# Maxima handed to the scores by halves, and the weighing moved between two pairs of matmuls, in an attention of 16 heads

## The chip, the cores and the metric

The kernel runs on one core of a Trainium2 chip. The metric is the device time of one launch in microseconds, the median of several runs; lower is better.

## What is computed

The program is a network of four blocks over x of 4 batches x 1024 tokens x 128 features: a gated linear recurrence with a feed-forward layer, a mixture of experts, an attention block, and a second attention block with a mixture of experts. The change touches the two attention blocks alone, which have one shape:

```python
q, k = rope(proj(Wq, bq)), rope(proj(Wk, bk))     # 4 batches, 16 heads, 1024 tokens, 8 features a head
v = proj(Wv, bv)
scores = einsum('bhtd,bhsd->bhts', q, k) / sqrt(8)
attn = softmax(scores, axis=-1)                   # over all 1024 keys, no mask
out = einsum('bhts,bhsd->bhtd', attn, v)          # 4 x 16 x 1024 x 8
y = out.reshape(B, T, 128) @ Wo + bo
```

Everything is float32 at the borders. Queries and keys are split into a high and a low part (three products of 8 features) and held as 25 rows, the 25th of which is the maximum of a query's scores on the query side and -1 on the key side, so that one matmul gives score minus maximum.

## The kernel before, in words

An attention block (called a layer here, there are two) has a stage for each batch, `attention_inputs`, which makes the 25-row parts of queries and keys and stores them to `qk_parts` in HBM, and then one stage, `attention`, for all batches. That stage works on 16 groups (`GROUPS`), each of 4 heads of one batch. A group's parts are loaded by SP into one of 4 slots of `qs` and `ks` (`load`, eight DMAs).

For each group two things are computed by TensorE (PE):

- **Maxima.** A unit (`max`, one head and one tile of 128 queries, 32 units a group) is two matmuls of 128 queries against 512 keys each (line 923), into a pair of PSUM banks. VectorE (DVE) reduces the 128 x 1024 scores to a column of `mx` (line 1043). There are two such pairs of banks, taken in turn by all work in the list `fills`: fill n waits until fill n-2 has been read (`ring`). When a group's maxima are there, `turn_max` transposes `mx` (line 930), DVE copies it to `m_row` (line 1048), and SP copies that to the 25th rows of `qs` (`store_maxima`, line 884).
- **Steps.** A step s takes one tile of 128 keys and 512 queries (a half) for the four heads: a group is 16 steps, 8 for each half. `score(s, j)` is one matmul (line 959) into one of 3 score banks; ScalarE (ACT) takes the exponential (line 1023) into `p`; `weigh(s)` multiplies the four heads' `p` by the values and a column of ones (line 969, four matmuls beside each other in column groups). The score matmul n waits until the exponential n-3 is done (line 957), the weighing of step s-1 until all exponentials of step s-1 are done (line 965).

The order on PE is written out by hand. Ahead of the steps stands a lead of `LEAD` units, the last 8 fills of it with an extra matmul (`WARM`, line 976). Then each step has two units, `one` and `two`, taken apart into their two matmuls and put between the scores; heads 0 and 1 lie in partitions 0 to 63, heads 2 and 3 in 64 to 127, so a score matmul and a unit's matmul of the other half of the partitions can run beside each other. The order of a step before is

```python
score(s,0) one(0) score(s,1) one(1) score(s,2) weigh(s-1) two(0) score(s,3) two(1) [turns]
```

where heads 0 and 1 of the scores stand next to unit heads 2 or 3 (`one`), and scores 2 and 3 next to unit heads 0 or 1 (`two`).

The turns are further fills of a single bank, behind a step's units, by the table `fill_plan`: `turn_max` of group g in step 16g-3; `turn_out` (four transposes of the weighed half, line 934, after ACT copied it out by `copy_out`, line 1008) in steps 16g+9 and 16g+17; at a batch's end two `turn_o` and, two steps later, two `project` (line 947), which DVE adds up (line 1063). `copy_out` of a half stands on ACT behind the third exponential of the first step of the next half and waits for the last weighing of the half.

At the stage's start SP waits for `parts_stored`, all stores of `qk_parts`, then loads three groups.

Of the kernel before, what the change touches and what calls it, by code (L numbers as in the profile page):

```python
# [5 lines left out]
F32 = mybir.dt.float32  # L6
# [8 lines left out]
P = 128  # L15
# [7 lines left out]
GH = 4  # L23
# [795 lines left out]
M_BANK, NM = 3, 2  # L819
O_BANK = 7  # L820
STEPS = NH * NT
LEAD = 40
WARM = 8
GROUPS = B * NG

# [1 line left out]
def fill_plan():  # L827

    plan = [[] for _ in range(GROUPS * STEPS + 8)]
    first = [("max", *divmod(u, UN)) for u in range(LEAD)]  # L830
    first.insert(UN, ("turn_max", 0, 0))
    for u in range(LEAD, GROUPS * UN):
        s = (u - LEAD) // 2
        plan[s].append(("max", *divmod(u, UN)))
    for g in range(GROUPS):
        if g:
            plan[STEPS * g - 3].append(("turn_max", g, 0))
        for h in range(NH):
            plan[STEPS * g + NT * (h + 1) + 1].append(("turn_out", g, h))
        if g % NG == NG - 1:  # L840
            s = STEPS * (g + 1)
            plan[s + 3] += [("turn_o", g // NG, h) for h in range(NH)]
            plan[s + 5] += [("project", g // NG, h) for h in range(NH)]
    return first, plan


def attention(nc, t, w, layer, a):
# [14 lines left out]
    with stage(nc, "loaded0", "loaded1", "loaded2", "loaded3", "row0", "row1", "filled", "used", "turned",  # L862
# [5 lines left out]
        @block.sync  # L868
        def _(sp):
            def load(g):  # L870
                if g >= NKF:
                    sp.wait_ge(scored, GH * STEPS * (g - NKF + 1))
                b, h0, n = g // NG, (g % NG) * GH, g % NKF
                for j in range(GH):
                    r = slice(GR * j, GR * j + ROWS_QK)
                    sp.dma_start(a["qs"][r, n, :].bitcast(F32), t["parts"][b, 0, h0 + j, :, :]).then_inc(loaded[n], 16)
                    sp.dma_start(a["ks"][r, n, j % KM, :].bitcast(F32), t["parts"][b, 1, h0 + j, :, :])\
                        .then_inc(loaded[n], 16)

            def store_maxima(g):  # L880
                sp.wait_ge(turned, g + 1)
                for j in range(GH):
                    r = GR * j + ROWS_QK - 1
                    sp.dma_start(a["qs"][r:r + 1, g % NKF, :].bitcast(F32).rearrange("r (i c) -> r i c", c=P),
                                 a["m_row"][NT * j:NT * (j + 1), g % 2, :].bitcast(F32)).then_inc(row[g % 2], 16)

            sp.wait_ge(t["parts_stored"], PART_STORES * 16 * B * (layer + 1))
            for g in range(3):
                load(g)
            for g in range(GROUPS):  # L890
                store_maxima(g)
                if g + 3 < GROUPS:
                    load(g + 3)

        @block.tensor
        def _(pe):
# [11 lines left out]
            def fill(f, parts=(0, 1)):  # L908
                kind, g, u = f
                n = number[f]  # L910
                if parts[0] == 0:
                    assert made[0] == n
                    made[0] += 1
                    bank = ring(n)
                else:
                    bank = M_BANK + 2 * (n % NM)
                if kind == "max":
                    i, j = place(u)
                    if u == 0 and parts[0] == 0:
                        pe.wait_ge(loaded[g % NKF], 16 * 2 * GH * (g // NKF + 1))  # L920
                    for h in parts:
                        r = slice(j // KM * KT, (j // KM + 1) * KT)
                        last = pe.matmul(psum[:, bank + h, :], a["qs"][r, g % NKF, i * P:(i + 1) * P],  # L923
                                         a["ks"][r, g % NKF, j % KM, h * HALF:(h + 1) * HALF], start=True, stop=True)
                    if parts[-1] == 1:
                        last.then_inc(filled, 1)
                elif kind == "turn_max":
                    done = number["max", g, UN - 1] + 1
                    pe.wait_ge(used, done - sum(by_act[:done]))
                    pe.transpose(psum[0:UN, bank, 0:P], a["mx"][:, g % 2, :], t["ident"][:, :]).then_inc(filled, 1)  # L930
                elif kind == "turn_out":
                    pe.wait_ge(out_copied, NH * g + u + 1)
                    for i in range(TPH):
                        last = pe.transpose(psum[:, bank, i * P:(i + 1) * P], a["o_raw"][:, u, i * P:(i + 1) * P],
                                            t["ident"][:, :])
                    last.then_inc(filled, 1)
                elif kind == "turn_o":
                    done = number["turn_out", NG * g + NG - 1, u] + 1
                    pe.wait_ge(used, done - sum(by_act[:done]))
                    for i in range(TPH):  # L940
                        last = pe.transpose(psum[:, bank, i * P:(i + 1) * P], a["o"][:, u * TPH + i, :], t["ident"][:, :])
                    last.then_inc(filled, 1)
                else:
                    pe.wait_ge(o_copied, NH * g + u + 1)
                    for i in range(TPH):
                        c = (u * TPH + i) * P
                        last = pe.matmul(psum[:, bank, i * P:(i + 1) * P], t["y_t"][:, c:c + P], w.att[layer][5],
                                         start=True, stop=True)
                    last.then_inc(filled, 1)

            def score(s, j):
                g, (h, i) = s // STEPS, divmod(s % STEPS, NT)
                n = GH * s + j
                if s % STEPS == 0 and j == 0:
                    pe.wait_ge(row[g % 2], 16 * GH * (g // 2 + 1))
                if n >= NS:
                    pe.wait_ge(exped, n - NS + 1)
                r = slice(j // KM * KT, (j // KM + 1) * KT)
                pe.matmul(psum[:, S_BANK + n % NS, :], a["ks"][r, g % NKF, j % KM, i * P:(i + 1) * P],  # L959
                          a["qs"][r, g % NKF, h * HALF:(h + 1) * HALF], start=True, stop=True).then_inc(scored, 1)  # L960
# [16 lines left out]
            for s in range(nsteps):  # L977
                todo = list(plan[s])
                one = todo.pop(0) if todo and todo[0][0] == "max" else None
                two = todo.pop(0) if todo and todo[0][0] == "max" else None  # L980
                score(s, 0)
                if one:
                    fill(one, (0,))
                score(s, 1)
                if one:
                    fill(one, (1,))
                score(s, 2)
                if s:
                    weigh(s - 1)
                if two:  # L990
                    fill(two, (0,))
                score(s, 3)
                if two:
                    fill(two, (1,))
                for f in todo:
                    fill(f)
# [6 lines left out]
        def _(act):  # L1003
# [6 lines left out]
            def copy_o(b):  # L1010
                for h in range(NH):
# [2 lines left out]
                    act.activation(t["y_t"][:, h * HALF:(h + 1) * HALF], psum[:, bank, :], ACT.Copy)\  # L1014
                        .then_inc(o_copied, 1)

            for s in range(nsteps):
                for j in range(GH):
                    n = GH * s + j
# [13 lines left out]
        def _(dve):  # L1033
            recips = 0
            for n, (kind, g, u) in enumerate(fills):
# [3 lines left out]
                dve.wait_ge(filled, n + 1)  # L1039
                if kind == "max":  # L1040
                    i, j = place(u)
                    c = NT * j + i
                    dve.tensor_reduce(a["mx"][:, g % 2, c:c + 1], psum[:, bank:bank + 2, :].rearrange("p a d -> p (a d)"),  # L1043
                                      AX.X, ALU.max).then_inc(used, 1)
                elif kind == "turn_max":
                    if g >= 2:
                        dve.wait_ge(row[g % 2], 16 * GH * (g // 2))
                    dve.tensor_copy(a["m_row"][:, g % 2, :], psum[0:UN, bank, 0:P]).then_inc(turned, 1)
                    dve.wait_ge(turned, g + 1)
                    dve.sem_inc(used, 1)  # L1050
                elif kind == "turn_out":
                    out = psum[:, bank, :].rearrange("p (i j c) -> p i j c", i=TPH, j=GH)
# [18 lines left out]
def build(nc, x_in, cols_in, rows_in, gates_in, ident_in, cos_in, sin_in, w0_in, wo_in, w1_in, w2_in,  # L1071
          att_in, gate_in, consts_in, moe0_in, moe1_in, out):
    with ExitStack() as ctx:
        names = {}

        def sb(name, shape, dt=F32, where=ctx):
            names[name] = names.get(name, 0) + 1
            return where.enter_context(nc.sbuf_tensor(f"{name}_{names[name]}", shape, dt))
# [147 lines left out]
        for layer in range(2):  # L1226
            with ExitStack() as scope:
                a = {}
                t["v_ext"] = sb("v_ext", [P, B * NT, HEADS * VE + VW - VE], where=scope)
                a["qs"] = sb("qs", [P, NKF, L], F32R, where=scope)  # L1230
                a["ks"] = sb("ks", [P, NKF, KM, L], F32R, where=scope)
                target = (x_all, n_all)[layer]
                with ExitStack() as inner:
                    t["cos"], t["sin"] = sb("cos", [P, L], where=inner), sb("sin", [P, L], where=inner)
# [32 lines left out]
                a["p"] = sb("p", [P, NP, HALF], where=scope)  # L1267
                a["o_raw"] = sb("o_raw", [P, NH, HALF], where=scope)
                a["o"] = t["x2"]
                a["mx"] = sb("mx", [P, 2, UN], where=scope)  # L1270
                a["m_row"] = sb("m_row", [UN, 2, P], F32R, where=scope)
                a["rs"] = sb("rs", [P, 2, TPH, GH], where=scope)
                a["sum"] = [view(target, b) for b in range(B)]
                attention(nc, t, w, layer, a)

# [96 lines left out]
```

## Time and profile before

| | us |
|---|---|
| median of 3 runs | 2943.95 |
| lowest and highest | 2941.54, 2946.24 |
| the profiled execution's own time | 2944.78 |
| its span, first to last instruction | 2943.5 |
| mean granted TensorE clock over the span | 0.867 |
| PE busy | 2323.2 (79%) |
| DVE busy | 2053.8 (70%) |
| ACT busy | 1479.5 (50%) |
| POOL busy | 503.9 (17%) |

The two attention stages cover about 793 to 1616 us and 1724 to 2547 us of the span. In the profile PEld is the loading of weights, which runs beside the matmuls; SPq is SP's queue, with a row for each DMA that it issues. A row's time is from its start to its end; instructions on one engine overlap in their pipelines, so that a period is read from start to start. A release in brackets names what ended an engine's idle time. A row of several instructions that overlap is merged (x2, x8).

### The profile page before, as it was taken

The page shows a single profiled execution, that of the slowest core. Times are in us where ns is not written, and L with a number is a line of the kernel's source. Part 1 is how long each engine was busy: PE and PEld are TensorE (multiplying, and loading weights), DVE is VectorE, ACT ScalarE, POOL GpSimd, SP SyncE. Part 2 cuts the span into 40 slices and gives each one's busy share as a digit, 9 for nine tenths or more (in the row PEclk, how much of TensorE's full clock was granted, in tenths as well). Part 3 has the DMA queues.
Part 4 walks back from the last instruction along what each step waited for, and adds up shares of the span by engine and source line. Part 5 has one row for each costly group of instructions (what it writes and reads, how often), then busy time and mean ns, then how long its engine had stood idle before and what let it go on. Part 6 is the DMA issues. An engine that isn't in the chain of part 4 may idle for free. (4 is left out here: it accounts for less than half of the span.)

```text
span 2943.5 us, 37846 instructions
## 1 busy us (share of the span) xinstructions
PE 2323.2 (79%) x13096; PEld 1285.4 (44%) x13096; DVE 2053.8 (70%) x3485; ACT 1479.5 (50%) x2898; POOL 503.9 (17%) x410
## 2 busy tenths in 40 slices
PE   6888856933399999999998559999999999639920
PEld 5667745721144444344443224444444443239920
DVE  6667657635578888888881667888888887266635
ACT  4443320411117777777777104777777777513510
POOL 2223301756400000000000320000000000005644
PEclk9999965966659999999999757999999999857965
DMA  4000010343300000000000320000000000201211
GB/s 165 0 0 0 0 35 18 99 69 114 115 25 12 23 17 19 24 12 24 12 1 5 125 90 12 24 20 16 23 12 24 12 12 1 79 22 50 69 49 50
DMA packets 65302, 109.11 MB, mean 37 GB/s; under 512 B 11120, under 2 KB 45040, under 8 KB 64880
## 3 DMA queue, kind: packets, MB, share of 16 engines
q1 hardware_dynamic: 56176, 88.60, 8.9%
q0 software_dynamic: 8960, 18.37, 2.9%
q8 instruction: 95, 1.56, 0.2%
q14 instruction: 71, 0.58, 0.1%
HBM read 64.46 MB, written 41.94 MB: 36 GB/s over the span
## 5 line engine op out<-in xcount | busy, mean ns | idle before, releaser
L1043 DVE TENSOR_REDUCE mx<-psum 128x1 f32<-128x1024 f32 x1024 | 1216.0, 1220 | 273.4 <-PE psum L923 273.4
L1023 ACT ACTIVATE p<-psum 128x512 f32<-128x512 f32 x2048 | 1086.5, 599 | 493.1 <-PE psum L959 486.4
L959 PE MATMUL psum<-qs,ks 64*128 64x512 f32 x2048 | 838.4, 453 | 13.5 <-ACT p L1023 13.0
L923 PE MATMUL psum<-ks,qs 64*128 64x512 f32 x2048 | 689.4, 461 | 81.7 <-DVE mx L1043 44.1
L923 PEld LDWEIGHTS psum<-ks,qs 64*128 64x128 f32 x2048 | 312.3, 195 | 565.8 <-DVE mx L1043 425.2
L969 PE MATMUL psum<-p,v_ext 128*32 128x512 f32 x4096 | 547.8, 607 | 1.4 <-ACT p L1023 1.4
L959 PEld LDWEIGHTS psum<-qs,ks 64*128 64x128 f32 x2048 | 368.6, 185 | 242.3 <-ACT p L1023 212.3
L157 PE MATMUL psum<-ident,xn 128*128 128x128 f32 x160 | 44.3, 454 | 264.1 <-DVE xn L125 219.8
L575 ACT ACTIVATE hid<-psum,stage 128x128 f32<-128x128 f32 x448 | 132.5, 367 | 181.4 <-PE psum L545 181.4
L519 POOL DMA_INDIRECT x_in<-n_rows,token_of x152 | 167.1, 1100 | 251.0 <-POOLq L78 183.7
L649 POOL COPY n_all<-xn 128x1024 f32 x4 | 4.2, 1040 | 883.4 <-DVE xn L132 883.4
L1261 POOL MEMSET v_ext<- 128x5344 f32 x2 | 9.1, 4552 | 839.7 <-POOLq L78 839.7
L615 POOL DMA_INDIRECT back<-answers,slot_of x128 | 132.8, 1037 | 100.0 <-issue 51.8
L157 PEld LDWEIGHTS psum<-ident,xn 128*128 128x128 f32 x160 | 29.4, 190 | 275.8 <-DVE xn L125 223.7
L545 PE MATMUL psum<-x_t,stage 128*128 128x128 f32 x896 | 137.4, 290 | 9.1 <-DVE x_t L584 6.2
L598 DVE COPY stage<-ew 128x642 f32 (+1 forms) x152 | 95.7, 630 | 69.2 <-DVE y_out L590 64.3
L969 PEld LDWEIGHTS psum<-p,v_ext 128*32 128x32 f32 x4096 | 81.0, 108 | 139.3 <-issue 119.4
L555 PE MATMUL psum<-stage,hid 128*128 128x128 f32 x896 | 126.3, 277 | 0.6 <-ACT hid L575 0.6
L545 PEld LDWEIGHTS psum<-x_t,stage 128*128 128x128 f32 x896 | 114.2, 195 | 25.5 <-DVE x_t L584 23.9
L229 PE MATMUL psum<-y_high,w_high 128*128 128x512 f32 x256 | 106.6, 416 | 20.5 <-PEq L78 20.5
L138 ACT ACTIVATE std<-var 128x8 f32<-128x8 f32 (+1 forms) x29 | 6.1, 210 | 219.8 <-DVE var L110 195.7
L555 PEld LDWEIGHTS psum<-stage,hid 128*128 128x128 f32 x896 | 113.6, 194 | 1.0 <-ACT hid L575 1.0
(171 smaller groups left out, 2378.2 us busy)
## 6 DMA issues: line engine op xcount, KB each, us to landing
qs<-qk_parts SPq DMA_DIRECT2D x128, 100.0 KB
ks<-qk_parts SPq DMA_DIRECT2D x128, 100.0 KB
answers<-y_out SPq DMA_DIRECT2D x152, 64.0 KB, 1.5
qk_parts<-qh SPq DMA_DIRECT2D x16, 512.0 KB, 4.5
qk_parts<-kh SPq DMA_DIRECT2D x16, 512.0 KB, 4.4
ew<-in_moe SPq DMA_DIRECT2D x1, 5136.0 KB, 18.1
ew<-in_moe SPq DMA_DIRECT2D x1, 4624.0 KB, 14.0
n_rows<-xn SPq DMA_DIRECT2D x8, 512.0 KB, 3.2
```

Of the source, the lines that this page charges most:

```text
L229: last = pe.matmul(psum[:, n % BANKS, :], a[:, m, c * P:(c + 1) * P], t[y][:, h * HALF:(h + 1) * HALF], start=(k == 0), stop=(k == 2))
L519: pool.indirect_dma_start(t["x_in"][:, i % NX, :], None, t["n_rows"], bass.IndirectOffsetOnAxis(ap=t["token_of"][:, i:i + 1], axis=0))\
L545: last = pe.matmul(psum[:, 2 + i % 2, f * P:(f + 1) * P], t["stage"][:, i % NST, W1 + f * P:W1 + (f + 1) * P], t["x_t"][:, i % 2, :], star ...
L555: last = pe.matmul(psum[:, 4 + i % 2, 0:P], t["hid"][:, i % 2, f, :], t["stage"][:, i % NST, W2 + f * P:W2 + (f + 1) * P], start=(f == 0), ...
L575: act.activation(t["hid"][:, i % 2, f, :], psum[:, 2 + i % 2, f * P:(f + 1) * P], func, bias=t["stage"][:, i % NST, B1 + f:B1 + f + 1]).th ...
L598: dve.tensor_copy(t["stage"][:, i % NST, :], t["ew"][:, bass.ds(e, 1), :] .rearrange("p a c -> p (a c)")).then_inc(staged, 1)
L615: pool.indirect_dma_start(t["back"][:, b % 2, i, k, :], None, t["answers"], bass.IndirectOffsetOnAxis(ap=t["slot_of"][:, b * NT + i, k:k + ...
L923: last = pe.matmul(psum[:, bank + h, :], a["qs"][r, g % NKF, i * P:(i + 1) * P], a["ks"][r, g % NKF, j % KM, h * HALF:(h + 1) * HALF], sta ...
L959: pe.matmul(psum[:, S_BANK + n % NS, :], a["ks"][r, g % NKF, j % KM, i * P:(i + 1) * P], a["qs"][r, g % NKF, h * HALF:(h + 1) * HALF], sta ...
L969: last = pe.matmul(psum[GR * j:GR * j + VW, O_BANK, :], t["v_ext"][:, b * NT + i, VE * (h0 + j):VE * (h0 + j) + VW], a["p"][:, (GH * s + j ...
L1023: act.activation(a["p"][:, n % NP, :], psum[:, S_BANK + n % NS, :], ACT.Exp, scale=DH ** -0.5)\
L1043: dve.tensor_reduce(a["mx"][:, g % 2, c:c + 1], psum[:, bank:bank + 2, :].rearrange("p a d -> p (a d)"), AX.X, ALU.max).then_inc(used, 1)
```

## The change

What it does:

- `LEAD` goes from 40 to 24 units. The 16 units stand in the steps instead, of which 244 now have two units each, before 236.
- `turn_max`, which was one transpose of 32 columns for a group, is two of 16 columns, one for each half of 512 queries: for the first half in step 16g-3, for the second in step 16g+5, and for group 0's first half in the lead. `m_row` has a place for each half, and each half's row goes by one DMA, before four for a group; each half's first score waits for its own row.
- `weigh(s-1)` stands ahead of `score(s, 2)`, before behind it.
- SP waits for `parts_stored` only ahead of the loads of the last batch, and ACT waits for it at the stage's start instead. `mx`, `m_row` and `rs` are allocated earlier, ahead of the inputs' stage.

```diff
-LEAD = 40
+LEAD = 24
+UH = UN // NH
...
-    first.insert(UN, ("turn_max", 0, 0))
+    first.insert(UH + 2, ("turn_max", 0, 0))
...
-        if g:
-            plan[STEPS * g - 3].append(("turn_max", g, 0))
+        for h in range(NH):
+            if g or h:
+                plan[STEPS * g + NT * h - 3].append(("turn_max", g, h))
...
+                if b == B - 1:
+                    sp.wait_ge(t["parts_stored"], PART_STORES * 16 * B * (layer + 1))
...
-            def store_maxima(g):
-                sp.wait_ge(turned, g + 1)
-                for j in range(GH):
-                    r = GR * j + ROWS_QK - 1
-                    sp.dma_start(a["qs"][r:r + 1, g % NKF, :].bitcast(F32).rearrange("r (i c) -> r i c", c=P),
-                                 a["m_row"][NT * j:NT * (j + 1), g % 2, :].bitcast(F32)).then_inc(row[g % 2], 16)
-
-            sp.wait_ge(t["parts_stored"], PART_STORES * 16 * B * (layer + 1))
+            def store_maxima(g, h):
+                sp.wait_ge(turned, NH * g + h + 1)
+                r = ROWS_QK - 1
+                sp.dma_start(a["qs"][r:P:GR, g % NKF, h * HALF:(h + 1) * HALF].bitcast(F32)
+                             .rearrange("r (i c) -> r i c", c=P), a["m_row"][:, h, :].bitcast(F32)).then_inc(row[h], 16)
+
             for g in range(3):
                 load(g)
             for g in range(GROUPS):
-                store_maxima(g)
+                for h in range(NH):
+                    store_maxima(g, h)
                 if g + 3 < GROUPS:
                     load(g + 3)
...
-                    done = number["max", g, UN - 1] + 1
+                    done = number["max", g, UH * (u + 1) - 1] + 1
                     pe.wait_ge(used, done - sum(by_act[:done]))
-                    pe.transpose(psum[0:UN, bank, 0:P], a["mx"][:, g % 2, :], t["ident"][:, :]).then_inc(filled, 1)
+                    pe.transpose(psum[0:UH, bank, 0:P], a["mx"][:, g % 2, UH * u:UH * (u + 1)], t["ident"][:, :])\
+                        .then_inc(filled, 1)
...
-                if s % STEPS == 0 and j == 0:
-                    pe.wait_ge(row[g % 2], 16 * GH * (g // 2 + 1))
+                if i == 0 and j == 0:
+                    pe.wait_ge(row[h], 16 * (g + 1))
...
-                score(s, 2)
                 if s:
                     weigh(s - 1)
+                score(s, 2)
...
+            act.wait_ge(t["parts_stored"], PART_STORES * 16 * B * (layer + 1))
...
-                    c = NT * j + i
+                    c = UH * (i // TPH) + TPH * j + i % TPH
...
-                    if g >= 2:
-                        dve.wait_ge(row[g % 2], 16 * GH * (g // 2))
-                    dve.tensor_copy(a["m_row"][:, g % 2, :], psum[0:UN, bank, 0:P]).then_inc(turned, 1)
-                    dve.wait_ge(turned, g + 1)
+                    if g:
+                        dve.wait_ge(row[u], 16 * g)
+                    dve.tensor_copy(a["m_row"][:, u, :], psum[0:UH, bank, 0:P]).then_inc(turned, 1)
+                    dve.wait_ge(turned, NH * g + u + 1)
```

The order of the instructions on PE in a plain step of the first layer, from one weighing (psum<-p) to the next; `ks,qs` is a unit's matmul and `qs,ks` a score. Before:

```order
L969 MATMUL psum<-p,v_ext 32x512 x4
L923 MATMUL psum<-ks,qs 128x512
L959 MATMUL psum<-qs,ks 128x512
L923 MATMUL psum<-ks,qs 128x512
L959 MATMUL psum<-qs,ks 128x512
L923 MATMUL psum<-ks,qs 128x512
L959 MATMUL psum<-qs,ks 128x512
L923 MATMUL psum<-ks,qs 128x512
L959 MATMUL psum<-qs,ks 128x512
L969 MATMUL psum<-p,v_ext 32x512 x4
```

And now:

```order
L973 MATMUL psum<-p,v_ext 32x512 x4
L963 MATMUL psum<-qs,ks 128x512
L926 MATMUL psum<-ks,qs 128x512
L963 MATMUL psum<-qs,ks 128x512
L926 MATMUL psum<-ks,qs 128x512
L963 MATMUL psum<-qs,ks 128x512
L926 MATMUL psum<-ks,qs 128x512
L963 MATMUL psum<-qs,ks 128x512
L926 MATMUL psum<-ks,qs 128x512
L973 MATMUL psum<-p,v_ext 32x512 x4
```

The third score of a step stood alone as the last matmul ahead of the weighing; it now follows it and is the first behind it.

The second place is SP's queue between two groups' maxima, in the first layer. Before:

```order
L884 DMA qs<-m_row 1x8x128 x4
L876 DMA qs<-qk_parts 25x1024
L877 DMA ks<-qk_parts 25x1024
```

And now:

```order
L887 DMA qs<-m_row 4x4x128 x2
L880 DMA qs<-qk_parts 25x1024
L881 DMA ks<-qk_parts 25x1024
```

Two DMAs of 4 rows x 4 tiles stand where four of one row stood, and the second of them waits for the second half's maxima, so the load of group g+3 behind it comes eight steps later.

## Rows read from the trace of the kernel before

**Rows 1.** Windows: stretch and length, busy us of each engine, PEclk the granted clock
```profile
805.10:865.60 60.50, 55.21 (x99) 23.53 (x99) 47.64 (x41) 0.00 (x0) 0.00 (x0) 0.50 0.10 39
...
869.70:1609.40 739.70, 711.27 (x4207) 293.96 (x4206) 578.86 (x553) 558.78 (x1055) 0.00 (x0) 1.00 0.04 15
```
**Rows 2.** Timeline of a plain step: start us, duration us, engine, line, what
```profile
1115.59 1.06 PE L969 MATMUL psum<-p,v_ext 128*32 128x512 f32 x8
...
1116.58 0.50 PE L959 MATMUL psum<-qs,ks 64*128 64x512 f32 x1
1116.91 0.39 PE L923 MATMUL psum<-ks,qs 64*128 64x512 f32 x1
...
1117.77 0.50 PE L959 MATMUL psum<-qs,ks 64*128 64x512 f32 x1
1118.20 0.64 PE L969 MATMUL psum<-p,v_ext 128*32 128x512 f32 x4
...
1117.12 0.60 ACT L1023 ACTIVATE p<-psum 128x512 f32<-128x512 f32 x1 [0.53 <-PE psum L959]
...
1117.34 2.35 DVE L1043 TENSOR_REDUCE mx<-psum 128x1 f32<-128x1024 f32 x2 [0.26 <-PE psum L923]
```
**Rows 3.** Timeline of the last step of the first layer, which has no units
```profile
1607.24 1.06 PE L969 MATMUL psum<-p,v_ext 128*32 128x512 f32 x8
1608.23 0.49 PE L959 MATMUL psum<-qs,ks 64*128 64x512 f32 x1
1609.41 0.64 PE L969 MATMUL psum<-p,v_ext 128*32 128x512 f32 x4 [0.69 <-ACT p L1023]
...
1608.76 0.60 ACT L1023 ACTIVATE p<-psum 128x512 f32<-128x512 f32 x1 [0.53 <-PE psum L959]
```
**Rows 4.** Timeline of two steps: ACT copies a half out, ahead of an exponential
```profile
1101.10 1.07 PE L969 MATMUL psum<-p,v_ext 128*32 128x512 f32 x8
...
1102.23 0.60 ACT L1008 ACTIVATE o_raw<-psum 128x512 f32<-128x512 f32 x1
1102.73 0.59 ACT L1023 ACTIVATE p<-psum 128x512 f32<-128x512 f32 x1
```
**Rows 5.** Timeline of PE in the step after it, with a turn (L934)
```profile
1103.80 1.07 PE L969 MATMUL psum<-p,v_ext 128*32 128x512 f32 x8
...
1105.46 0.66 PE L934 MATMUL psum<-ident,o_raw 128*128 128x128 f32 x4
...
1106.85 0.49 PE L923 MATMUL psum<-ks,qs 64*128 64x512 f32 x1 [0.30 <-DVE mx L1043]
...
1107.18 0.39 PE L923 MATMUL psum<-ks,qs 64*128 64x512 f32 x1
1107.41 0.39 PE L959 MATMUL psum<-qs,ks 64*128 64x512 f32 x1
...
1107.74 0.64 PE L969 MATMUL psum<-p,v_ext 128*32 128x512 f32 x4
```
**Rows 6.** Timeline of a batch's projection: the next step's first pair, DVE's second sum
```profile
1071.36 0.50 PE L959 MATMUL psum<-qs,ks 64*128 64x512 f32 x1
...
1071.46 0.69 DVE L1063 TENSOR_TENSOR x_all<-psum,x_all 128x512 f32<-128x512 f32 x1 [0.65 <-PE psum L947]
```
**Rows 7.** Timeline of the lead of the first layer: begin, and around its turn
```profile
805.11 1.23 PE L923 MATMUL psum<-ks,qs 64*128 64x512 f32 x4 [18.94 <-DMA ks<-qk_parts]
...
846.87 0.37 PE L930 MATMUL psum<-ident,mx 128*32 128x128 f32 x1 [1.41 <-DVE mx L1043]
847.17 1.22 PE L923 MATMUL psum<-ks,qs 64*128 64x512 f32 x2
...
849.47 0.79 PE L923 MATMUL psum<-ks,qs 64*128 64x512 f32 x1
```
**Rows 8.** Timeline at the stage's start: ACT's first work, SP's first load
```profile
792.98 1.28 ACT L1023 ACT_TABLE_LOAD   x1 [3.81 <-PEq L78]
...
796.31 0.33 SPq L876 DMA_DIRECT2D qs<-qk_parts  x1
```

More of the change, by code:

```diff
@@ L1231, in build @@
                 a["ks"] = sb("ks", [P, NKF, KM, L], F32R, where=scope)
+                a["mx"] = sb("mx", [P, 2, UN], where=scope)
+                a["m_row"] = sb("m_row", [UH, NH, P], F32R, where=scope)
+                a["rs"] = sb("rs", [P, 2, TPH, GH], where=scope)
                 target = (x_all, n_all)[layer]
@@ L1269, in build @@
                 a["o"] = t["x2"]
-                a["mx"] = sb("mx", [P, 2, UN], where=scope)
-                a["m_row"] = sb("m_row", [UN, 2, P], F32R, where=scope)
-                a["rs"] = sb("rs", [P, 2, TPH, GH], where=scope)
                 a["sum"] = [view(target, b) for b in range(B)]
```

## The prediction

> **What bounds the kernel now.** I read the windows first, cut at the two parts of the first attention stage (the second runs alike, so each price counts twice). The lead, from the first unit to the first score, takes 60.5 us with ACT idle, at a granted clock of 0.50, the lower level of 1.2 GHz; the 255 periods from the first weighing to the last take 739.7 us at 1.00, which is 2.4 GHz [rows 1]. PE's records cover 711 of these 739.7 us, which looks like a stage bound by PE. The timeline of a plain step says otherwise. Its period is 2.61 us (weighing at 1115.59, next at 1118.20) [rows 2], and the steps at the end of the layer, which have no units at all, still stand far apart: there one sees a weighing at 1607.24, its score matmul at 1608.23, the exponential from 1608.76 to 1609.36 and the weighing that needs it at 1609.41 [rows 3]. So the step is bound by a loop through PE and ACT, with four hops: weighing to the next score 0.99, score to exponential 0.53, exponential 0.60, its end to what waited 0.05 [rows 3]. In the program before, what waited is the third score, and the weighing starts 0.43 behind it (1117.77, 1118.20) [rows 2]. 0.99 + 0.53 + 0.60 + 0.05 + 0.43 = 2.60: the loop accounts for the whole period. DVE has 0.26 idle in a step [rows 2].
>
> A second kind of step has a turn. There the ring of two PSUM bank pairs has lost a place, and the next unit's first matmul waits for a reduce (0.30 idle, at 1106.85): the period is 1107.74 - 1103.80 = 3.94 us [rows 5]. A third kind holds the copy of a half on ACT, with 1103.80 - 1101.10 = 2.70 [rows 4, 5]. Counted in the plan of fills, the 255 periods are 43 with a turn, 31 with a copy and 181 others: 43 x 3.94 + 31 x 2.70 + 181 x 2.61 = 725.5. The other 14 us lie in three batch ends and the first step, at the low clock.
>
> **The weighing, moved.** The third score's bank comes free with exponential 4 of the step before, for which the weighing waits too. Before, that score went first, so ACT had three exponentials to do under the 0.99 us of the weighing. Now it has two (about 1.0 us), and the third and fourth come behind the weighing. The loop is now: weighing to third score 0.99, to its exponential 0.53, a pitch of 0.50 to the fourth exponential (the pitch of rows 4, 1102.23 to 1102.73, for two of this size), 0.60 for that, 0.05 to the weighing: 2.67. The fourth score isn't late: it is issued 0.33 behind the third, as line 923 at 1116.91 is now behind 1116.58 [rows 2], less than the pitch. So a plain step goes from 2.61 to 2.67, and saving PE a matmul buys nothing there. 160 periods x 0.06 = +9.6 us a layer.
>
> Where a half is copied out, the copy stands on ACT between the third and the fourth exponential. Before, the fourth had to wait for its score, and all but 0.09 of the copy was hidden (2.70 against 2.61). Now both exponentials come behind the weighing, and its whole pitch of 0.50 lies in the loop: 3.17 against 2.70. 31 x 0.47 = +14.6. The last period of the layer grows by one pitch, +0.5.
>
> In a step with a turn the exponentials are long done, and PE's own chain counts: blocked first matmul 1106.85, then 1107.18, the lone third score 1107.41, the weighing 1107.74 [rows 5]. That score leaves this place: -0.23. 43 x 0.23 = -9.9.
>
> **Why the pairs were made, weighed against this.** The trace shows what is saved: a score beside a unit's matmul costs PE no slot of its own (1107.41 - 1107.18 = 0.23 is the slot of the lone one) [rows 5]. The Trainium skill (TensorEngine Tiling, section Tiling Modes, Key Properties) says that tiles operate independently and in parallel, which speaks for pairing. By that rule alone each step would lose 0.23; by the loop above only the turn steps do. That case is the first rival.
>
> **The maxima by halves.** 16 more turns a layer. Behind units, where they cost: turns go from 43 to 60, of which 3 fall in the step of a batch's projection, so 14 plain steps become turn steps: 3.94 - 0.23 - 2.61 = +1.10 each, +15.4. In the projection's step a third extra fill means that the next unit waits for the second sum, done at 1071.46 + 0.69 = 1072.15, and 0.05 more, instead of starting at 1071.36 [rows 6]: +0.84 - 0.23 = +0.61, three times, +1.8; the three steps of turn_o lose 0.23 each, -0.7. The turns in the last 12 steps, which have no units, are free under the loop. The row goes by one DMA where four stood behind each other, and has three steps, some 8 us, until the score that needs it: no gain, since the four were in time, and no loss unless a single DMA takes longer than four did. The load of a group moves eight steps later, still some 30 steps ahead of its first unit: nothing.
>
> Sum of the steps: 9.6 + 14.6 + 0.5 - 9.9 + 15.4 + 1.8 - 0.7 = +31.3 a layer, +63 in all.
>
> **The lead.** Before: 32 units at (847.17 - 805.11 - 1.41 - 0.30) / 32 = 1.26 us, the turn with its idle 1.7, then 8 units with an extra matmul at 849.47 - 847.17 = 2.30 [rows 7]: 60.4, which is the window's [rows 1]. Now: 17 units at 1.26 (21.4), one at 2.30, the turn with its extra matmul about 0.30 + 1.15, six at 2.30: 39.0. The turn waits for unit 15 with two units behind it, so its idle of 1.41 goes. -21.5 a layer, -43. That counts the units out of the lead; into the steps they bring only the turns counted above, since a plain step has the same 2.67 with units or without. The granted clock is 0.50 over the lead and 1.00 over the steps [rows 1]; the extra matmuls stand ahead of the steps as before, so I take that it rises at the same place beside them, with ends of -3 and +5 us a layer.
>
> **The loads** start without the wait for the stores, by at most 796.31 - 792.98 = 3.3 us, the time by which ACT is ahead of SP's first load [rows 8]; the last stores still fill the queues, so 0 is the other end and I take -2.5, -5 in all. ACT's new wait lies under the lead.
>
> **Sum.** The profiled execution took 2944.8, 0.85 above the median of the runs: 2944.8 + 63 - 43 - 5 = **2959**.
>
> **Rivals.** Where they fall out: 0.2% is 5.9 us, about what a measurement tells from no change.
>
> 1. PE's stream is the bound and every step loses 0.23 (the skill's rule above, as a mechanism of this kernel). Then plain 160 x -0.23, copies 31 x -0.23, turns as above: -37 a layer, and 2944.8 - 75 - 48 = 2822. DVE's 2.35 [rows 2] would just fit in 2.38. For it: PE's 711 of 739.7. Against it: rows 3, where steps without units go no faster. 10%.
> 2. The loop stays as long as before: ACT gets its scores in time, since the score behind the weighing overlaps more of it, and the copy stays hidden. Plain and copy steps then cost nothing: -9.9 + 15.4 + 1.1 = +6.6 a layer, 2944.8 + 13 - 48 = 2910. It decides if the weighing lets a score through 0.06 sooner, and for the copy 0.5 sooner. Against it: 0.99 stands in each of rows 2 and 3. 17%.
> 3. The weighing follows a pair by 0.43, as it follows a lone score in rows 2, not by the 0.33 of rows 5. Then turn steps save 0.10 less (57 of them) and plain and copy steps are bound by the second pair, which waits for the third exponential, if its unit's matmul starts half a slot behind its score: 0.99 + 0.53 + 0.60 + 0.05 + 0.11 + 0.43 = 2.71 in a plain one. 57 x 0.10 + 191 x 0.04 = 13 us a layer: 2985. The skill (TensorEngine Tiling, the same section) says that a change of the tiling mode drains TensorE, which would be the cause; no row here separates it. A clock that rises well behind the first step would end in the same direction. 16%.
>
> **Numbers.** Forecast 57%, with 2940 to 2978 of its own (loads, clock and the prices' 0.02). Rivals 10, 17 and 16%. The range reaches down to rival 2 and up to rival 3: 2905 to 2990; rival 1 and the tails, under 2 in 10, are out. Faster by over 0.2%: rivals 1 and 2 and a sliver of the forecast, 0.30; within 0.2%, 0.10; slower, 0.60.
>
> **What would show it.** Plain periods of 2.67 with ACT's gap of about 0.7 us now between the second and third exponential; 3.17 where a half is copied; 3.71 with a turn, and 60 of these a layer; a lead of 39 us; 255 periods in 771 us. Plain periods of 2.4 would make it wrong altogether, and copies at 2.7 would take 29 us off.

## The result, and the profile after

The change is slower by 0.7%: 2963.51 us, the median of 4 runs (2962.48 to 2965.20), against 2944.26 of before in the same measurement (2941.54 to 2946.24), a ratio of 1.0067 (95% interval 1.0049 to 1.0084). Forecast was 2959. A second measurement (experiment 7) gave 1.0080 (1.0064 to 1.0096). The profiled execution took 2963.84 us, 19.1 more than that of before.

The windows of the changed kernel, cut like [rows 1] at the first layer's lead (first unit to first score, at 842.70) and at both layers' periods from first to last weighing (stretch and length, busy us of PE, PEld, DVE, ACT, POOL, the granted clock, then the DMA engines' share and GB/s):

```profile
804.10:842.70 38.60, 35.97 (x65) 15.64 (x65) 28.66 (x25) 0.00 (x0) 0.00 (x0) 0.50 0.10 39
847.20:1620.70 773.50, 690.53 (x4261) 263.27 (x4259) 602.80 (x586) 554.95 (x1057) 0.00 (x0) 1.00 0.04 15
1788.50:2560.70 772.20, 689.17 (x4257) 262.64 (x4255) 602.84 (x586) 554.87 (x1057) 0.00 (x0) 1.00 0.04 15
```

The reader is to see three things. The lead is 38.6 where it was 60.5. The steps are 773.5 where they were 739.7. And PE is busy for 690.5 us of them where it was for 711.3: by its records PE is spared 21 us, and the steps of this layer became 34 us longer (32 in the second).

A plain step, answering to [rows 2] (timeline: start, duration, engine, line; a row "..." stands for rows left out):

```profile
1084.94 1.07 PE L973 MATMUL psum<-p,v_ext 128*32 128x512 f32 x8
1085.94 0.49 PE L963 MATMUL psum<-qs,ks 64*128 64x512 f32 x1
...
1087.12 0.50 PE L963 MATMUL psum<-qs,ks 64*128 64x512 f32 x1
1087.12 0.49 PE L926 MATMUL psum<-ks,qs 64*128 64x512 f32 x1
1087.61 1.07 PE L973 MATMUL psum<-p,v_ext 128*32 128x512 f32 x8
```

ACT over this step and the next, which holds a copy (line 1012), answering to [rows 4], and PE's weighings around that copy:

```profile
1086.47 2.07 ACT L1028 ACTIVATE p<-psum 128x512 f32<-128x512 f32 x4 [0.60 <-PE psum L963]
1089.14 0.60 ACT L1028 ACTIVATE p<-psum 128x512 f32<-128x512 f32 x1 [0.60 <-PE psum L963]
1089.63 0.59 ACT L1012 ACTIVATE o_raw<-psum 128x512 f32<-128x512 f32 x1
1090.11 1.58 ACT L1028 ACTIVATE p<-psum 128x512 f32<-128x512 f32 x3
```

```profile
1090.76 1.07 PE L973 MATMUL psum<-p,v_ext 128*32 128x512 f32 x8 [0.47 <-ACT p L1028]
```

The plain period is 1087.61 - 1084.94 = 2.67. ACT's gap lies where it was forecast, ahead of the third exponential (1086.47, 0.53 behind its score at 1085.94); it is 0.60 long, where about 0.7 was forecast. In the next step the third exponential starts at 1089.14, the copy follows, the fourth starts only at 1090.11, and the weighing waits for it until 1090.76: 1090.76 - 1087.61 = 3.15.

The turn step of maxima (line 933), answering to [rows 5]:

```profile
1078.54 1.06 PE L973 MATMUL psum<-p,v_ext 128*32 128x512 f32 x8
...
1080.20 0.28 PE L933 MATMUL psum<-ident,mx 128*16 128x128 f32 x1
...
1081.62 0.50 PE L926 MATMUL psum<-ks,qs 64*128 64x512 f32 x1 [0.71 <-DVE mx L1048]
...
1081.96 0.39 PE L926 MATMUL psum<-ks,qs 64*128 64x512 f32 x1
1082.28 1.07 PE L973 MATMUL psum<-p,v_ext 128*32 128x512 f32 x8
```

The period is 3.74 us (1078.54 to 1082.28), where it was 3.94. The transpose itself takes 0.28; what makes the step 1.07 longer than a plain one is the next unit's first matmul, which is held until 1081.62 by the reduce before (1080.34 to 1081.57).

### The profile page after: what moved, and what is told of

The parts are those of the page before. It is cut to its first block and busy times, and to the rows that moved or that the text cites. A ratio compares the mean times of both kernels' runs of the same rounds, so it can differ in the third digit from the quotient of the medians.

```text
span 2962.6 us, 38016 instructions
## 1 busy us (share of the span) xinstructions
PE 2236.9 (76%) x13128; PEld 1204.4 (41%) x13128; DVE 2063.2 (70%) x3517; ACT 1470.3 (50%) x2898; POOL 504.2 (17%) x410
## 5 line engine op out<-in xcount | busy, mean ns | idle before, releaser
L926 PE MATMUL psum<-ks,qs 64*128 64x512 f32 x2048 | 787.1, 468 | 99.6 <-DVE mx L1048 63.7
L963 PE MATMUL psum<-qs,ks 64*128 64x512 f32 x2048 | 780.0, 454 | 70.8 <-ACT p L1028 43.5
L963 PEld LDWEIGHTS psum<-qs,ks 64*128 64x128 f32 x2048 | 337.0, 185 | 672.9 <-ACT p L1028 642.1
L926 PEld LDWEIGHTS psum<-ks,qs 64*128 64x128 f32 x2048 | 338.2, 191 | 171.3 <-DVE mx L1048 121.2
## 6 DMA issues: line engine op xcount, KB each, us to landing
ew<-in_moe SPq DMA_DIRECT2D x1, 4624.0 KB, 14.6
```

## The experiments

Where times matter an experiment is compared with before in the same measurement, on one chip, as a ratio; in the three measurements of the experiments (1 to 4; 6 to 9; 5 and 10), on three chips, before itself took 2970.3, 2950.7 and 2950.5 us. The steps of the change, profiled in two measurements, agreed within 0.2 us a layer, so periods are compared directly. A change of the clock in single steps, shown at the end, can move a layer's steps by 1 to 2 us. "Steps" are the us from a layer's first weighing to its last: before 739.7 and 740.1, the change 773.5 and 772.2.

**1. The weighing back.**

```diff
-                if s:
-                    weigh(s - 1)
                 score(s, 2)
+                if s:
+                    weigh(s - 1)
```

> The changed kernel with the weighing back behind the third score; halves, lead of 24 and loads stay. Loop theory: the plain step returns to 2.61 us, the copy step to 2.70, the turn step to 3.94 and the one with a projection and a turn to about 5.9. Per layer against before: 17 more turns in steps with units (14 x 1.32 + 3 x 0.9 = 21), the lead 21.5 shorter, the loads about 1: 2944 - 2 - 1, so about 2942 and no difference from before. If PE's stream were the bound and the pairs a gain, this would be slower than the change, above 2964.

Measured: ratio 0.9994 (0.9985 to 1.0003). Plain period 2.61, copy 2.70, turn 3.93, projection with a turn 5.88; steps 761.0 and 761.1. As expected, halves, the shorter lead and the earlier loads together can't be told from nothing: up to the first weighing the lead gives 21.0 us a layer (64.6 to 43.6), and the 17 new turns in steps with units take 21.3 and 21.0. The whole loss of the change is the weighing's place.

**2. The weighing alone**, in the kernel before (the same lines moved the other way, `weigh(s - 1)` ahead of `score(s, 2)`).

> The kernel before with nothing but the weighing moved ahead of the third score. Loop theory: plain steps 2.61 to 2.67, copy steps 2.70 to 3.16, turn steps 3.94 to 3.74, lead unchanged: 173 x 0.055 + 31 x 0.46 - 43 x 0.19 + 0.5 = 16 us a layer, 2944 + 32 = 2976. Rival (the loss of the change lies in the halves): no more than 2950.

Measured: ratio 1.0097 (1.0081 to 1.0112), some 28 us. Steps 753.2 and 754.0, so +13.5 and +13.9; expected were 16, which left out that the steps of turn_o and of the projection lose 0.2 each and that the first period shortens (4.01 to 2.67 in the first layer, 4.07 to 3.50 in the second). PE is busy for less and the layer is longer:

```profile
890.30:1643.50 753.20, 677.63 (x4208) 261.20 (x4207) 579.79 (x554) 553.14 (x1057) 0.00 (x0) 1.00 0.04 14
```

PE's busy time in the steps falls from 711.3 [rows 1] to 677.6. With PE's work in pairs and its lead unchanged, the steps grow; that refutes the first rival by itself.

**3. The copy one exponential earlier.**

```diff
-                    if j == 2 and s and s % NT == 0:
+                    if j == 1 and s and s % NT == 0:
```

> The changed kernel with the copy of a half on ACT behind the second exponential instead of the third. Loop theory: the copy then falls in ACT's gap between second and third exponential, waits for the weighing's end, and only about 0.1 us of it stays in the loop: the copy step goes from 3.16 to about 2.76 us, 31 a layer, so 2963.5 - 25 = 2939. If the copy step's length came from the copy's place in PSUM or from something else than ACT's order, it stays at 3.16 and the time at 2963.

Measured: ratio 0.9987 (0.9978 to 0.9996), so this one edit takes the change from slower than before to a little faster. Every copy period is 2.76. ACT in such a step of this kernel, behind the weighing at 982.91:

```profile
984.05 0.60 ACT L1012 ACTIVATE o_raw<-psum 128x512 f32<-128x512 f32 x1 [0.20 <-PE psum L973]
984.54 2.06 ACT L1028 ACTIVATE p<-psum 128x512 f32<-128x512 f32 x4
```

The copy waits for the weighing's end (984.05), and the third exponential starts at 984.54, 0.63 behind its score at 983.91 instead of 0.53. So 0.1 of the copy is left in the loop. Steps 759.7 and 759.6, against 773.5 and 772.2: 26 us for both layers, 25 were expected. 1.6 of the 26 are the clock in the change's first layer, shown at the end.

**4. SP waits for all stores.**

```diff
+            sp.wait_ge(t["parts_stored"], PART_STORES * 16 * B * (layer + 1))
             for g in range(3):
                 load(g)
```

(and the wait ahead of the last batch's loads goes; ACT's wait at the stage's start stays)

> The changed kernel with SP waiting for all stores ahead of its first load, as before. The traces of before and of the change show the first unit about 1.4 us sooner after the inputs' end; so this should be 1 to 3 us a layer slower than the change: 2965 to 2969. The rival, that loads in the queue behind stores gain nothing: 2963.5.

Measured: ratio 1.0086 (1.0073 to 1.0100) beside 1.0067 and 1.0080 of the change in the two other measurements: by times not to be told apart. By traces, from the last store's issue to the first unit, 13.97 and 12.96 us here, 12.27 and 12.11 in the change, 13.70 and 13.71 before. The direction is as expected, 0.9 to 1.7 us a layer. The traces of all runs, but for experiment 6, which fills a tile first, put it more firmly: with SP's wait (before, experiments 2 and 4) the six layers lie between 12.96 and 14.20, mean 13.65; without it sixteen layers lie between 11.92 and 12.45, mean 12.19. The earlier loads gain 1.5 us a layer. The trace of the change, SP first, shows why it isn't more:

```profile
791.85 0.52 SPq L725 DMA_DIRECT2D qk_parts<-kh  x1
793.41 0.94 SPq L880 DMA_DIRECT2D qs<-qk_parts  x1
...
804.13 1.22 PE L926 MATMUL psum<-ks,qs 64*128 64x512 f32 x4 [17.51 <-DMA ks<-qk_parts]
```

The first load goes out 1.6 us behind the last store, where it was 4.9, but the first unit, which needs all eight loads of its group, follows 10.7 us after it (804.13 - 793.41), where it took 8.8 (805.11 [rows 7] - 796.31 [rows 8]). Of the 3.3 us, 1.9 are given back in this layer, and in the second 1.35 of 3.0. Part of it goes in issuing: in the first layer the eighth load is issued 3.8 us behind the first, where it was 2.4. That the stores, still under way, are the cause is the likely reading; no run separates it.

**5. Four DMAs for a half's row.**

```diff
-                r = ROWS_QK - 1
-                sp.dma_start(a["qs"][r:P:GR, ...
+                for j in range(GH):
+                    r = GR * j + ROWS_QK - 1
+                    sp.dma_start(a["qs"][r:r + 1, ...
```

(the counts that PE and DVE wait for on the row are changed to match)

> The changed kernel with each half's row stored by four DMAs, one a head, in place of one. If the landing is covered by the three steps between turn and score: every period as in the change (first score of a half not late) and the steps of a layer at 773 us. If the single DMA is what brings the row in time: the period ahead of each half's first score grows by up to 2 us, 31 times a layer.

Measured, one run: steps 771.7 and 771.4, no period ahead of a half's first score longer than in the change (2.66 to 2.67). The expected 773 was the change's first layer; the difference is the clock in its last steps, which did not fall here. The row's DMA was covered with four and is with one; by these periods that part of the change does nothing to the time.

**6. Exponentials of half the columns.**

```diff
-                    act.activation(a["p"][:, n % NP, :], psum[:, S_BANK + n % NS, :], ACT.Exp, scale=DH ** -0.5)\
+                    act.activation(a["p"][:, n % NP, 0:HALF // 2], psum[:, S_BANK + n % NS, 0:HALF // 2],
+                                   ACT.Exp, scale=DH ** -0.5)\
```

(Besides, GpSimd fills `p` with ones in a short stage ahead of each attention, once the stores are done, so the first unit comes some 7 us later.)

> The changed kernel with exponentials of 256 of the 512 columns; the other half of the weights stays at 1, set once a layer by a fill of some us (so the softmax is left out for half of the queries). Loop theory: the plain step holds two exponentials, so it falls from 2.67 by about 2 x 0.2 us, until DVE's two reduces (2.35) bound it: 2.3 to 2.4. Theory that PE's own stream bounds the plain step: it stays at 2.67.

The kernel leaves out the softmax of half of the queries. Measured, one run: plain periods of 2.40 and 2.47 in turn, 2.43 in the mean; steps 719.4 and 718.9. PE does all of its work in 2.43 us, so its stream doesn't bound the step of 2.67. What bounds it now is DVE: five reduces with no idle time between them, 6.09 / 5 = 1.22 each, so two take 2.44. The expected 2.3 to 2.4 took the 2.35 of a merged row of two for their pitch.

```profile
1098.01 6.09 DVE L1048 TENSOR_REDUCE mx<-psum 128x1 f32<-128x1024 f32 x5
```

The turn step stays at 3.74: there the ring counts, not ACT.

**7. The change once more.**

> The change itself, once more, beside the kernels of this call and before on one chip. It should be 19 to 21 us above before, as on record; the times of the first four experiments are then read against before, 1.0097 for the weighing alone being more than this.

Measured: 1.0080 (1.0064 to 1.0096), 23.7 us by the medians. That is more than the 19 to 21 expected, which lie at the low end of the interval (19 to 28 us). Steps 773.3 and 772.1, as in the change, so what is more does not lie in them; experiment 2's 1.0097 is read beside this.

**8. Turns in pairs, weighing back.** The weighing's lines as in experiment 1, and

```diff
         for h in range(NH):
-            plan[STEPS * g + NT * (h + 1) + 1].append(("turn_out", g, h))
+            late = 4 if h == 0 or g % NG != NG - 1 else 0
+            plan[STEPS * g + NT * (h + 1) + 1 + late].append(("turn_out", g, h))
```

> Weighing back behind the third score, and each transpose of the output moved four steps later, into the step that has a transpose of maxima: two turns in one step, two such steps a group instead of four with one turn. Theory that a turn costs by the place that it takes in the ring of two: two fills in one step keep the ring's phase, so a double step takes about 4.5 us against 2 x 3.94 - 2.61 = 5.27: some 45 to 50 us less than with the weighing back alone, ratio to before about 0.983. Theory that each turn costs its own time: no gain, ratio 0.999.

Measured: ratio 0.9841 (0.9827 to 0.9854), 46 us less than before. PE in such a double step:

```profile
979.96 1.07 PE L974 MATMUL psum<-p,v_ext 128*32 128x512 f32 x8
...
981.61 0.66 PE L939 MATMUL psum<-ident,o_raw 128*128 128x128 f32 x4
983.00 0.28 PE L934 MATMUL psum<-ident,mx 128*16 128x128 f32 x1 [0.73 <-DVE mx L1049]
...
984.38 1.07 PE L974 MATMUL psum<-p,v_ext 128*32 128x512 f32 x8
```

4.42 us for a step with both turns, 0.49 more than one with a single turn. The first turn takes a place in the ring and shifts it; the second shifts it back, and its own wait (until 983.00) is the one that the next unit had before. Steps 738.1 in both layers, 23 less than in experiment 1, 46 in all, as expected: a turn costs by its place in the ring far more than by its work.

**9. Turns in pairs, early copy**, with the weighing where the change has it.

> The changed kernel with the copy of a half behind the second exponential and the turns in pairs. Double step about 4.3 us against 2 x 3.74 - 2.67 = 4.81, copy step 2.76: about 30 us less than with the early copy alone, ratio to before about 0.989. If turns cost each their own time: 0.999.

Measured: ratio 0.9860 (0.9845 to 0.9875). Double step 4.23 (4.3 expected), copy 2.76, plain 2.67; steps 743.7 and 744.2. That is 15 to 16 us a layer less than in experiment 3, 31 in both, where about 30 were expected; the ratio is lower than the expected 0.989, by some 9 us, which the steps do not account for. By the steps the weighing between the pairs still loses against behind the third score, by 6 us a layer, with the other costs out of the way.

**10. The pairs with a lead of 22.**

```diff
-LEAD = 24
+LEAD = 22
```

> The version with the turns in pairs and the weighing back, with a lead of 22 units instead of 24, the shortest for which unit 15 of a group still stands a step ahead of its turn. Two units of 1.26 us less in each lead: 2.5 us a layer, 5 in all, ratio to before about 0.982. If a transpose of maxima now waits for its reduce, the double step grows by up to 1 us and the gain is lost: 0.99.

Measured: ratio 0.9815 (0.9801 to 0.9828), the best here and 1.8% faster than the kernel before. From first unit to first weighing it takes 41.1 us against 43.6 of experiment 8, and the double step stays at 4.42. The traces account for 6 us in both layers together (5 expected); the intervals of 8 and 10 touch.

## Why the prediction was right

Before and after, in us of the profiled executions: from first unit to first weighing -43.0, steps +33.8 and +32.1, loads -1.4 and -1.6, -0.8 over the rest of the program: +19.1. Forecast were -43, +31.3 twice and -5: +14.6. (The terms as printed in the forecast's last sum, 2944.8 + 63 - 43 - 5, add up to 2959.8; 2959 has the 0.85 taken off by which that execution lay above the median.) Point by point:

- **The loop through PE and ACT bounds a plain step, not PE.** Right. Forecast 2.67, measured 2.67; experiment 6 halves the exponentials and the period falls to 2.43 with PE's work unchanged, experiment 2 takes PE's work away and the period grows. Over all plain steps the mean went from 2.615 to 2.667, so the term is 0.05, not 0.06, a step: 1 us a layer less than forecast. As a calculation from hops (0.99, 0.53, 0.50, 0.60, 0.05) it was exact to 0.01.
- **The copy comes out of its cover.** Right: forecast 3.17, measured 3.15 to 3.16, 31 a layer. Experiment 3 shows the cause, the copy's place in ACT's order. It is the largest single term of what the weighing's place costs, 14 us a layer.
- **The turn steps.** Forecast 3.71, measured 3.73 to 3.74, since the reduce that holds the ring starts 0.03 later (1080.34, 1.80 behind the weighing, before 1105.57, 1.77). 57 times, +1.6 us a layer: with 1.6 us of the clock in one layer, the small miss of the steps. A transpose of the output in a step without units, priced at nothing, took 2.90 where a plain one takes 2.66, once a layer. The projection with a turn was forecast at the old 5.02 plus 0.61, 5.63, and took 5.68.
- **The lead.** Forecast 39.0 and -21.5; measured 38.6 and -21.9 from first unit to first score (804.13 to 842.70; before 805.11 to 865.57), and -21.5 to the first weighing (43.1 against 64.6). That the last agrees with the forecast is in part luck, by the next point. The clock came back some 4 us behind the first weighing, as before.
- **ACT's new wait** lies under the lead, as was said, but what stood behind it does not. ACT's table load (1.28 us), done at the stage's start before (792.98 [rows 8]), now comes behind the first score at 842.70:

```profile
843.58 1.28 ACT L1028 ACT_TABLE_LOAD   x1 [53.97 <-PE psum L963]
844.88 3.06 ACT L1028 ACTIVATE p<-psum 128x512 f32<-128x512 f32 x6
```

  The first exponential starts 2.17 us behind the first score, where it was 0.83. It is so in both layers of all ten runs that have the wait, and not in before and experiment 2, which have not; with the order of before (experiment 1) the first weighing follows the first score by 5.02 instead of 4.14. So the change lost 0.9 us a layer by a term that the forecast had at nothing; in the change itself the earlier weighing of the first step hides half of it (4.52). A run without the wait was not made.
- **The loads** were mis-sized: -2.5 a layer forecast, -1.5 measured (experiment 4: 0.9 to 1.7). More of the 3.3 us is given back before the first unit than the forecast allowed.
- **Nothing for the row's DMA:** right, by experiment 5.
- **Rival 1**, PE's stream as the bound, which gave 2822: refuted by experiments 2 and 6. The Trainium skill's rule (TensorEngine Tiling, section Tiling Modes, Key Properties) that tiles work in parallel is borne out by the trace, with score and unit both at 1087.12 and PE 21 us less busy in a layer. It tells what PE is spared, not what the step gains.
- **Rival 2**, the old loop kept: refuted by each plain period and by the copy's 3.15.
- **Rival 3**, a weighing 0.43 behind a pair: not where it would have cost. In turn steps the weighing follows the unit's matmul by 0.32 (1081.96 to 1082.28), as forecast. In plain steps it stands 0.49 behind the pair (1087.12 to 1087.61). In the plain step this costs nothing, as the fourth exponential ends just ahead, at 1087.57 by its pitch and length. Whether the 0.49 is a wait for that exponential or PE's own stays open; with shorter exponentials (experiment 6) 0.43 was left from score to weighing (1101.91 to 1102.34). That a change of the tiling mode causes it no run shows.

## What to carry to other kernels

A step's period is the longest loop over its engines; write its hops down from a step that has nothing else in it, and ask of a reordering which hops it puts into the loop, before counting what it spares an engine that is 96% busy by its records. Work that hides in a gap of an engine (here the copy between the third and the fourth exponential) has to move with the gap. In a ring of two, an extra fill costs by the phase that it shifts (here 1.3 us for one in a step, 1.8 for two): put such fills in pairs. After adding a wait, look at what stood behind it on that engine: here a table load of 1.28 us went from the stage's start to the first score.

## What the runs showed of the hardware that was not expected

In the first layer of the change, in the steps behind the last unit, the granted clock fell and came back. The rows are the first 3 us from the weighing ahead of the transpose of the output (line 938) that stands alone there, in the first and in the second layer:

```profile
1600.22:1603.22 3.00, 3.00 (x15) 1.46 (x16) 0.26 (x1) 2.02 (x4) 0.00 (x0) 0.80 0.00 0
2541.85:2544.85 3.00, 3.00 (x20) 1.26 (x24) 0.55 (x2) 2.17 (x5) 0.00 (x0) 1.00 0.00 0
```

The granted clock was 0.51, the lower level, from 1602.5 to 1605.5, and 1.00 up to 1602 and again in the microsecond behind 1605.5. Two periods took 3.76 and 3.37 us, where the second layer has 2.90 and 2.66 in the same place: 1.6 us in all. It came again in the first layer of experiment 7 and in the second layer of experiment 4, on two chips; in the other layers of experiments 4 and 7, and in both of experiment 5, whose steps there are the same, it did not: three layers of eight. In all eight PE was busy for 8.16 or 8.17 of the 10 us ahead of that weighing, at a clock of 1.00. In the kernel before it was busy for less in the same place, 8.11 us, and in experiment 2 for 7.71, and the clock did not fall in either. So PE's busy time ahead of it does not tell the layers with the fall from those without; what does stays open.
